# Fixed addresses for the 64 row scatters of a routing stage, in place of a loop that copies their row numbers first

## The chip, the core and the metric

The kernel runs on one core of a Trainium2 chip. The metric is the device time of one execution in microseconds (us), as the median of several runs. The core has five engines with a program each: TensorE (PE, matrix products), VectorE (DVE), ScalarE (ACT), GpSimd (POOL) and SyncE (SP, which here only issues DMAs). They wait for one another through semaphores.

## What is computed

A decoder of two layers on 32 sequences of 128 tokens of width 256. Layer 0 has a gated recurrence, a retention block and a mixture of experts; layer 1 has attention, cross attention on a context, and a memory layer. The change lies in the dispatch of the mixture of experts. Cut to that, the reference is:

```python
logits = xt @ wg                                   # 4096 tokens, 8 experts
scores = softmax(logits)
topv, topi = top_k(scores, 2)
flat = one_hot(topi.T, 8).reshape(2 * N, 8)
pos = sum((cumsum(flat, axis=0) - 1) * flat, -1).reshape(2, N).T
valid = pos < capacity                             # 1024 rows an expert
disp = zeros((8, capacity, 256)).at[topi, where(valid, pos, 0)].add(xt * valid)
y = relu(disp @ w1 + b1) @ w2 + b2                 # per expert
out = sum(gate * y[topi, pos], over the 2 choices)
...
Q = q @ Wq + bq; K = ctx @ Wk + bk; V = ctx @ Wv + bv    # cross attention of layer 1
```

## The kernel before

The work goes in 16 units of two sequences (UNITS = 16, UB = 2). Each stage is a software pipeline over the units: `pipelined` calls a step function per unit, the first ones written out, the rest in a hardware loop that is unrolled 2 or 4 times. `done`, `landed` and `landed4` are waits on semaphores; a DMA adds 16 to its semaphore when it has landed. The order of the work is written by hand, one program for each engine.

**Stage A** computes recurrence, retention and the routing logits, and stores its result x2 to HBM. **The routing stage** follows. VectorE (`r_vector`) turns the logits into a row number of `disp_d` for every token and choice, and writes these into `slot_s` (128 partitions x 2 choices x 32 sequences, L928); tokens over the capacity get a number beyond the bound. Then GpSimd (`r_gpsimd`) does 16 groups, one a unit. A group has four scatters (L1016), one for each of two choices and two sequences; a scatter writes 128 rows of 1 KB from `R["x"]` to the rows of `disp_d` that the numbers name.

**Beside it** run the keys and values of layer 1's cross attention, which need nothing of the routing: SyncE loads a context tile (L995), TensorE transposes it (`to_feature`, L469) and multiplies it by two weights (L477, L485), ScalarE copies the results (L974, L978, L979) and SyncE stores them (L1000). VectorE splits the first expert's weights into parts (L1166, L499, L1170).

**SyncE's program** (`r_sync`) ties the two together. Its step for unit t is, in this order: wait until the context tile of t-2 is transposed and load the context of t; wait for the scatters of unit t-4 (`r_sc`), whose buffer of four is then free, and load x2 of t (L997); wait for ScalarE's copies of t-2 and store its keys and values. SyncE's queue is in order, so one late wait holds up all that follows. After the last step comes `m_sync`, the expert stage: it waits for all 64 scatters (L1072) and loads the first tile of `disp_d` (L1078).

**The expert stage** M runs 16 tiles of 512 rows. TensorE waits in its beginning for all stores of keys and values, then for the first tile, transposes it (L1118), and goes on with the products (L504). Nothing of it can start before the last scatter has landed.

The program of the routing stage on GpSimd, on which the change bears:

## Time and profile before

| | us |
|---|---|
| median of 3 runs | 1977.65 |
| lowest and highest run | 1974.51, 1977.91 |
| the profiled execution, its own time | 1973.47 |
| span in its trace | 1971.7 |
| PE, DVE, ACT, POOL busy | 1629.6, 1272.4, 744.0, 525.7 |

The span runs from the first to the last instruction in the trace; 1.8 us of the execution lie around it. Busy time of an engine is an average over stages with different limits, so the rows below are read by stage: stage A ends at about 375 us, the routing stage reaches to about 490 us, the expert stage to about 880 us.

### The profile page before, as it was taken

The numbers are of one execution on the slowest core, as the hardware profiler recorded it, in microseconds if no ns is written. First come the engines' busy times: TensorE is split into PE (matmuls) and PEld (weight loads), VectorE is DVE, ScalarE is ACT, GpSimd is POOL, SyncE is SP. The second block draws the span as 40 slices with busy tenths as digits, with TensorE's granted clock in tenths as the row PEclk, the third lists the DMA queues.
The fourth block names the chain that finished last, engine by engine and source line by source line (L and its number), as shares of the span: only waits on it lengthen the run. The fifth ranks groups of instructions, "written<-read, shape, count | busy, mean of one in ns | idle before, by whom it ended". The sixth has DMA issues, their size and how long they took to land.

```text
span 1971.7 us, 35134 instructions
## 1 busy us (share of the span) xinstructions
PE 1629.6 (83%) x12950; PEld 1429.1 (72%) x12950; DVE 1272.4 (65%) x2542; ACT 744.0 (38%) x1319; POOL 525.7 (27%) x648
## 2 busy tenths in 40 slices
PE   4667777575999999985777769999968999899997
PEld 3556656464898888874566558887847889888897
DVE  4879999620555555525988837876756666665664
ACT  3334444132444444431333324443423333333332
POOL 1223232176000000005555311111103333333333
PEclk8878898698899999997999969999979999999999
DMA  4331110385022222302222231111110000000000
GB/s 164 118 118 33 37 42 26 129 269 206 29 86 86 86 85 91 112 27 86 65 68 82 65 134 61 64 59 55 34 33 1 22 23 12 23 17 17 22 12 17
DMA packets 98603, 133.92 MB, mean 68 GB/s; under 512 B 8562, under 2 KB 83548, under 8 KB 97956
## 3 DMA queue, kind: packets, MB, share of 16 engines
q1 hardware_dynamic: 87716, 107.21, 16.4%
q0 software_dynamic: 6144, 16.41, 2.6%
q10 hardware_dynamic: 4608, 8.39, 1.2%
q8 instruction: 98, 1.61, 0.3%
q14 instruction: 37, 0.30, 0.1%
HBM read 82.02 MB, written 50.33 MB: 67 GB/s over the span
## 4 chain that ended last, share of the span: by engine, by line
PE 31%; issue 11%; DVE 8%; POOL 4%; ACT 1%; DVEq 0%; POOLq 0%; DMA 0%; ACTq 0%
PE psum L504 11%; PE psum L1656 3%; PE psum L1640 3%; POOL d_g_parts L1919 3%; PE psum L1634 2%; PE psum L1617 2%; PE psum L485 2%; PE psum L477 2%; PE psum L1317 1%; DVE arena_y L455 1%; PE psum L469 1%; DVE arena_y L1435 1%; PE psum L1343 1%; DVE arena_y L1429 1%; POOL arena_y L1280 1%
## 5 line engine op out<-in xcount | busy, mean ns | idle before, releaser
L1919 POOL TENSOR_TENSOR d_g_parts<-arena_x,d_g_parts 128x512 fp32r<-128x512 f32 x128 | 164.6, 1286 | 306.4 <-ACT d_g_parts L2010 306.4
L504 PE MATMUL psum<-d_x_parts,d_v_high 128*128 128x256 f32 x1024 | 198.4, 292 | 27.9 <-DVE arena_x L2126 24.8
L504 PE MATMUL psum<-d_v_high,d_g_parts 128*128 128x256 f32 x1024 | 205.9, 284 | 13.0 <-POOL d_g_parts L1919 13.0
L504 PE MATMUL psum<-m_w_high,m_h_parts 128*128 128x256 f32 x1024 | 188.0, 284 | 0.0
L504 PEld LDWEIGHTS psum<-d_x_parts,d_v_high 128*128 128x128 f32 x1024 | 159.9, 193 | 38.7 <-DVE arena_x L2126 28.3
L2126 DVE SCALAR_TENSOR_TENSOR arena_x<-arena_x,psum 128x512 f32<-128x512 f32 x128 | 87.7, 685 | 143.9 <-ACT arena_x L2018 143.7
L504 PEld LDWEIGHTS psum<-d_v_high,d_g_parts 128*128 128x128 f32 x1024 | 167.8, 191 | 16.4 <-POOL d_g_parts L1919 16.2
L1144 ACT ACTIVATE arena_x<-psum,b_e 128x512 f32<-128x512 f32 x128 | 88.2, 689 | 196.5 <-PE psum L504 94.2
L504 PE MATMUL psum<-m_xF_parts,m_w_high 128*128 128x512 f32 x512 | 159.6, 393 | 2.1 <-DVE m_xF_parts L499 2.1
L504 PEld LDWEIGHTS psum<-m_w_high,m_h_parts 128*128 128x128 f32 x1024 | 160.8, 192 | 0.0
L469 PE MATMUL psum<-const,arena_x 128*128 128x128 f32 x448 | 78.8, 312 | 81.1 <-DVE arena_x L455 40.3
L504 PE MATMUL psum<-d_x_parts,d_vd_low 128*128 128x256 f32 x512 | 145.4, 284 | 0.0
L504 PE MATMUL psum<-m_w_low,m_h_parts 128*128 128x256 f32 x512 | 144.9, 283 | 0.0
L504 PE MATMUL psum<-d_vu_low,d_g_parts 128*128 128x256 f32 x512 | 144.6, 282 | 0.0
L2018 ACT ACTIVATE arena_x<-psum 128x512 f32<-128x512 f32 x128 | 76.5, 597 | 177.5 <-PE psum L504 177.5
L469 PEld LDWEIGHTS psum<-const,arena_x 128*128 128x128 f32 x448 | 58.5, 160 | 104.2 <-DVE arena_x L455 46.9
L499 DVE TENSOR_TENSOR m_h_parts<-arena_x,m_h_parts 128x512 fp32r<-128x512 f32 x128 | 84.5, 687 | 44.0 <-ACT m_h_parts L1148 44.0
L504 PEld LDWEIGHTS psum<-m_xF_parts,m_w_high 128*128 128x128 f32 x512 | 96.1, 190 | 21.8 <-issue 2.5
L1709 ACT ACTIVATE arena_x<-psum,arena_x 128x1024 f32<-128x1024 f32 x64 | 71.1, 1110 | 100.8 <-PE psum L1640 100.8
L1286 POOL COPY c_idx_t<-slot_g 128x4 int32<-128x4 int32 (+1 forms) x16 | 2.9, 181 | 395.8 <-POOLq L356 395.8
L1767 DVE TENSOR_REDUCE arena_x<-psum 128x16 f32<-128x2048 f32 x32 | 73.3, 2290 | 53.8 <-PE psum L1617 53.8
L2010 ACT ACTIVATE d_g_parts<-arena_x 128x512 fp32r<-128x512 f32 x128 | 80.1, 626 | 67.4 <-DVE arena_x L2131 67.4
(270 smaller groups left out, 4000.5 us busy)
## 6 DMA issues: line engine op xcount, KB each, us to landing
arena_y<-in_L_ffn_w SPq DMA_DIRECT2D x16, 1024.0 KB, 7.9
arena_x<-x_d SPq DMA_DIRECT2D x48, 256.0 KB, 2.8
arena_x<-in_ctx SPq DMA_DIRECT2D x32, 256.0 KB, 4.0
disp_d<-zeros ACTq DMA_DIRECT2D x32, 256.0 KB, 2.7
x_d<-arena_x SPq DMA_DIRECT2D x32, 256.0 KB, 2.1
kv_d<-arena_x SPq DMA_DIRECT2D x16, 512.0 KB, 3.5
arena_x<-disp_d SPq DMA_DIRECT2D x16, 512.0 KB, 8.5
y_d<-arena_x SPq DMA_DIRECT2D x16, 512.0 KB, 9.3
```

The lines of the kernel that those rows point to most:

```text
L469: ins = nc.tensor.transpose(dst[:, c * T + b * S:c * T + (b + 1) * S], src[:, b, c * P:(c + 1) * P], ident)
L499: return nc.vector.tensor_tensor(dst, src, high.bitcast(F32), ALU.subtract)
L504: ins = nc.tensor.matmul(dst, left[a_], right[b_], start=start and k == 0, stop=stop and k == 2, skip_group_check=True)
L1144: nc.scalar.activation(M["hr"][:, m % 4, :], bank(2 + m % 4), ACT.Relu, bias=b1_e[:, (u.c // 2) % 2, m:m + 1]).then_inc(m_hs, 1)
L1640: ins = nc.tensor.matmul(bank(4 + quad % 2)[:, j * S:(j + 1) * S], X["k"][rows, u.p, par, c * T + b * S:c * T + (b + 1) * S], X["q"][rows, ...
L1656: ins = nc.tensor.matmul(bank(7)[32 * quad:32 * quad + 32, (kind * NC_ + c) * S:(kind * NC_ + c + 1) * S], left, X["eT"][:, b, at:at + S], ...
L1709: nc.scalar.activation(X["eT"][:, b, half * 1024:(half + 1) * 1024].rearrange("p (q n) -> p q n", q=2), psum[:, 4:6, :], ACT.Exp, scale=HD ...
L1767: nc.vector.tensor_reduce(X["mx"][:, b, :].rearrange("p (q j) -> p q j", q=4)[:, :, 0:4], psum[:, 0:4, :].rearrange("p q (k s) -> p q k s" ...
L1919: nc.gpsimd.tensor_tensor(K["gP"][:, s % 2, 1], K["g"][:, s % 2], K["gP"][:, s % 2, 0].bitcast(F32), ALU.subtract).then_inc(d_gl, 1)
L2010: nc.scalar.activation(K["gP"][:, s % 2, 0], K["g"][:, s % 2], ACT.Copy).then_inc(d_gh, 1)
L2018: nc.scalar.activation(K["th"][:, s % 2], bank(s % 2).rearrange("p (k t) -> p k t", k=2), ACT.Tanh, scale=0.5).then_inc(d_th, 1)
L2126: nc.vector.scalar_tensor_tensor(K["t"][:, s % 2], K["th"][:, s % 2], 1.0, z, ALU.add, ALU.mult).then_inc(d_t, 1)
```

## The change

The loop over the units is written out in full. The row numbers are no longer copied into a small tile `R["idx"]`: each scatter reads them where they are, in `slot_s`, which a loop whose position is only known in a register did not do. With the copy go its semaphore `r_idx`, the two `carry` operations around it (one addition of one element each, which give the waits ahead of them an instruction to stand on), and GpSimd's own wait for the scatters of unit t-4. That this wait isn't needed for the buffer follows from SyncE's: x2 of t is loaded into it only when the scatters of t-4 have landed.

```diff
         R["x"] = arena_x.take([P, 4, UB, D])
-        R["idx"] = arena_x.take([P, 4, TOP0, UB]).bitcast(I32)
...
-            def step(t):
-                landed4(pool, r_in, t)
-                landed4(pool, r_sc, t.back(4), 4)
-                carry(pool, 0)
-                nc.gpsimd.tensor_copy(R["idx"][:, t.c % 4], slot_s[:, :, bass.ds(t.n * UB, UB)]).then_inc(r_idx, 1)
-                done(pool, r_idx, t)
-                carry(pool, 1)
+            for u in (Unit(0, n, 4) for n in range(UNITS)):
+                landed4(pool, r_in, u)
                 for c in range(TOP0):
                     for b in range(UB):
+                        at = u.n * UB + b
                         nc.gpsimd.indirect_dma_start(
                             out=disp_d,
-                            out_offset=bass.IndirectOffsetOnAxis(ap=R["idx"][:, t.c % 4, c, b:b + 1], axis=0),
-                            in_=R["x"][:, t.c % 4, b, :], in_offset=None, bounds_check=SLOTS - 1,
-                            oob_is_err=False).then_inc(r_sc[t.c % 4], 16)
-            pipelined(pool, UNITS, 0, step, unroll=4)
+                            out_offset=bass.IndirectOffsetOnAxis(ap=slot_s[:, c, at:at + 1], axis=0),
+                            in_=R["x"][:, u.c % 4, b, :], in_offset=None, bounds_check=SLOTS - 1,
+                            oob_is_err=False).then_inc(r_sc[u.c % 4], 16)
```

GpSimd's order of instructions at the start of the routing stage, before (`r_in_0` is the load of the unit's x2, `r_slots` the end of VectorE's work on the numbers, `s_prefill` the zeroing of `disp_d`):

```order
L463 TENSOR_TENSOR A_st<-A_st,minus_half 128x2 [waits ln2_ag] x2
L513 TENSOR_TENSOR pool_cell<-pool_cell 1x1 [waits r_in_0,r_slots,s_prefill]
L1011 COPY arena_x<-slot_s 128x4
L513 TENSOR_TENSOR pool_cell<-pool_cell 1x1 [waits r_idx]
L1016 DMA disp_d<-arena_x 8192x256 x4
L513 TENSOR_TENSOR pool_cell<-pool_cell 1x1 [waits r_in_1]
L1011 COPY arena_x<-slot_s 128x4
L513 TENSOR_TENSOR pool_cell<-pool_cell 1x1 [waits r_idx]
L1016 DMA disp_d<-arena_x 8192x256 x4
```

The same place of GpSimd's program in the changed kernel, whose scatter is its line 1010:

```order
L463 TENSOR_TENSOR A_st<-A_st,minus_half 128x2 [waits ln2_ag] x2
L1010 DMA disp_d<-arena_x,slot_s 8192x256 [waits r_in_0,r_slots,s_prefill]
L1010 DMA disp_d<-arena_x,slot_s 8192x256 x3
L1010 DMA disp_d<-arena_x,slot_s 8192x256 [waits r_in_1]
L1010 DMA disp_d<-arena_x,slot_s 8192x256 x3
L1010 DMA disp_d<-arena_x,slot_s 8192x256 [waits r_in_2]
L1010 DMA disp_d<-arena_x,slot_s 8192x256 x3
```

Three instructions have gone ahead of each four scatters, and the first wait now stands on the first scatter itself.

A quarter of the loop's body on GpSimd before, with the branch at its end (ISA and REGISTER_ALU work out the address of the copy and the values waited for):

```order
L513 TENSOR_TENSOR pool_cell<-pool_cell 1x1 [waits r_sc_3,r_in_3]
L1011 ISA
L1011 COPY arena_x<-slot_s 128x4
L182 REGISTER_ALU
L513 TENSOR_TENSOR pool_cell<-pool_cell 1x1 [waits r_idx]
L1016 DMA disp_d<-arena_x 8192x256 x4
L171 REGISTER_ALU
L171 COMPARE_AND_BRANCH
L329 UNCONDITIONAL_BRANCH
```

The end of GpSimd's routing stage in the changed kernel:

```order
L1010 DMA disp_d<-arena_x,slot_s 8192x256 [waits r_in_2]
L1010 DMA disp_d<-arena_x,slot_s 8192x256 x3
L1010 DMA disp_d<-arena_x,slot_s 8192x256 [waits r_in_3]
L1010 DMA disp_d<-arena_x,slot_s 8192x256 x3
L329 UNCONDITIONAL_BRANCH
```

Copies, additions, address work and loop branch are gone there, and no scatter waits for an earlier scatter any more. The programs of the other four engines have the same instructions in the same order as before.

## Rows read from the trace of the kernel before

**Rows 1.** The page's first line.

```profile
span 1971.7 us, 35134 instructions
```

**Rows 2.** Busy time by stretch, heading included: routing numbers, scatters, start of M.

```profile
core 0: us, PE busy (x) PEld busy (x) DVE busy (x) ACT busy (x) POOL busy (x), PEclk, DMA share, GB/s
375.00:392.60 17.60, 6.67 (x15) 3.73 (x16) 13.74 (x32) 2.87 (x5) 0.00 (x0) 0.60 0.88 313
392.60:489.40 96.80, 65.84 (x310) 53.98 (x309) 13.03 (x24) 25.18 (x46) 72.25 (x112) 0.92 0.70 242
489.40:498.50 9.10, 1.94 (x8) 1.57 (x8) 1.37 (x3) 1.09 (x2) 0.00 (x0) 0.50 0.43 139
```

**Rows 3.** Timeline of all engines, 488 to 499: start, duration, idle before, its releaser.

```profile
488.35 0.97 POOL L1016 DMA_INDIRECT disp_d<-arena_x  x1 [0.30 <-issue]
490.70 6.15 SPq L1078 DMA_DIRECT2D arena_x<-disp_d  x3
494.51 1.94 PE L1118 MATMUL psum<-const,arena_x 128*128 128x128 f32 x8 [18.74 <-DMA arena_x<-disp_d]
498.55 1.19 PE L504 MATMUL psum<-m_xF_parts,m_w_high 128*128 128x512 f32 x2 [2.10 <-DVE m_xF_parts L499]
```

**Rows 4.** Timeline, GpSimd's first group of scatters.

```profile
392.62 0.24 POOL L513 TENSOR_TENSOR pool_cell<-pool_cell 1x1 f32<-1x1 f32 x1 [22.28 <-DVE slot_s L928]
393.07 0.52 POOL L513 TENSOR_TENSOR pool_cell<-pool_cell 1x1 f32<-1x1 f32 x1
393.98 1.22 POOL L1016 DMA_INDIRECT disp_d<-arena_x  x1 [0.38 <-issue]
```

**Rows 5.** Timeline, one group of GpSimd's loop and the next one's first instruction.

```profile
465.49 0.18 POOL L513 TENSOR_TENSOR pool_cell<-pool_cell 1x1 f32<-1x1 f32 x1
...
466.60 1.02 POOL L1016 DMA_INDIRECT disp_d<-arena_x  x1 [0.55 <-issue]
467.92 0.97 POOL L1016 DMA_INDIRECT disp_d<-arena_x  x1 [0.30 <-issue]
...
470.46 0.97 POOL L1016 DMA_INDIRECT disp_d<-arena_x  x1 [0.30 <-issue]
471.45 0.18 POOL L513 TENSOR_TENSOR pool_cell<-pool_cell 1x1 f32<-1x1 f32 x1
```

**Rows 6.** Everything on line 1016: the 64 scatters, in ns, and their landings.

```profile
L1016 POOL DMA_INDIRECT disp_d<-arena_x x64: 967/974/1488, 394.0 to 488.4; - x64
DMA to landing us min/median/max: 2.2/2.9/4.9
```

**Rows 7.** SyncE's waits from 395 to 480: total, times, longest.

```profile
SPq L997 <- DMA disp_d<-arena_x: 34.8, 10, 4.5
SPq L1000 <- ACT arena_x L979: 26.4, 10, 6.0
```

**Rows 8.** Keys and values: TensorE's transposes of units 3, 7, 15, SyncE's loads and stores.

```profile
401.71 0.66 PE L469 MATMUL psum<-const,arena_x 128*128 128x128 f32 x4 [1.62 <-DMA arena_x<-in_ctx]
422.49 0.66 PE L469 MATMUL psum<-const,arena_x 128*128 128x128 f32 x4 [2.10 <-DMA arena_x<-in_ctx]
468.20 0.66 PE L469 MATMUL psum<-const,arena_x 128*128 128x128 f32 x4 [1.50 <-DMA arena_x<-in_ctx]
468.50 0.37 SPq L997 DMA_DIRECT2D arena_x<-x_d  x1
L1000 SPq DMA_DIRECT2D kv_d<-arena_x x16: 337/368/374, 397.3 to 476.9; - x16
```

**Rows 9.** Landing times of the context loads of line 995.

```profile
DMA to landing us min/median/max: 2.7/4.1/11.3
```

**Rows 10.** Busy time by stretch, columns as in Rows 2: the most loaded one.

```profile
400.00:410.00 10.00, 8.31 (x41) 6.70 (x40) 6.08 (x11) 3.26 (x6) 7.63 (x10) 1.00 0.89 299
```

**Rows 11.** Groups from 392.6 to 489.4: busy us, mean ns.

```profile
L1016 POOL DMA_INDIRECT disp_d<-arena_x x64 | 63.7, 996 | 23.0 <-issue 23.0
L1166 DVE CAST m_piece<-arena_y 128x512 fp32r<-128x512 f32 x8 | 4.1, 513 | 0.2
```

**Rows 12.** Busy time by stretch: TensorE's clock around its return.

```profile
480.00:490.00 10.00, 0.00 (x0) 0.00 (x0) 0.00 (x0) 0.00 (x0) 7.16 (x10) 0.50 0.20 78
500.00:502.00 2.00, 2.00 (x6) 1.61 (x5) 0.00 (x0) 0.45 (x1) 0.00 (x0) 0.50 0.00 0
502.00:504.00 2.00, 2.00 (x8) 1.56 (x8) 0.69 (x1) 1.21 (x3) 0.00 (x0) 0.77 0.00 0
```

1 line of the change is left out of this document (removed).

## The prediction, made before the changed kernel ran

> **What bounds the kernel now.** I read three views in this order. First, busy time by stage, from which the reader is to see whose work fills each stretch. While VectorE works out the row numbers (375 to 392.6 us) GpSimd does nothing. From 392.6 to 489.4 the scatters run: GpSimd is counted busy for 72.25 of 96.8 us, TensorE for 65.84, VectorE for 13.03, and the DMA engines have a share of 0.70 [rows 2]. No engine is full, so the stretch is a chain of steps.
>
> Second, the timeline at its end, which names the chain. The last scatter starts at 488.35 and ends at 489.32; SyncE's first load of the dispatched rows is issued at 490.70; TensorE's first transpose starts at 494.51, after 18.74 us in which it had nothing to do; the first product starts at 498.55 [rows 3]. TensorE's work on keys and values had ended at 494.51 - 18.74 = 475.8, and the last store of keys and values was issued at 476.9, ending at 477.2 [rows 8]. So on the day of this trace only the scatters hold the expert stage: what they finish earlier, it starts earlier, until SyncE's own earlier work, which ends at 477.2, is the next to be late. That is 490.70 - 477.2 = 13.5 us away, and this number matters below.
>
> Third, the timeline of GpSimd. A group of four scatters with its preparation takes 471.45 - 465.49 = 5.96 us [rows 5]. Sixteen of them fill 489.32 - 392.62 = 96.7 us [rows 3, 4]; the first three are slower. Between groups there is no wait: the copy and the two additions follow each other and the scatters at once, so GpSimd runs its own chain from end to end, and its pace is the cost of its instructions.
>
> **The change part by part.** *Inside the loop.* One scatter follows the other after 0.30 us of "issue" and lasts 0.97 us: a pitch of 1.27 us, as from 467.92 to 470.46, two pitches in 2.54 [rows 5]. The gap between the last scatter of a group and the first of the next is 466.60 - 465.49 + 0.01 = about 1.12 us. The two additions and the copy lie in it. Without them it should be the 0.30 that stands between any two scatters; the first scatter of a group also lasts 1.02 in place of 0.97. Saved: 0.82 + 0.05 = 0.87 us at each of 15 boundaries, 13.0 us.
>
> *At the start.* The first addition starts at 392.62, when VectorE has delivered the numbers, and the first scatter at 393.98, 1.36 us later [rows 4]. The new first scatter waits for the same thing; give it the ordinary 0.30 of issue and it starts at 392.92. Saved: 1.06 us.
>
> *What is added.* Each group's first scatter now carries the wait for its x2 itself. No scatter of this trace does that. Bounded from below by nothing, since the wait is long satisfied (x2 of unit 15 is requested at 468.50 [rows 8], its scatters begin some 16 us later). Bounded from above by the largest issue gap ahead of a scatter in the loop, 0.55 against 0.30 [rows 5]: 0.25 x 15 = 3.8 us. I take 0.03 a group, 0.5 us in all, near the lower end, because such a wait is a check of a value that is already there. Reading the numbers out of `slot_s` costs what reading them out of the copy cost: one number a partition both times. Writing the loop out costs nothing that I can see: the first four groups were written out before too, and in them scatters follow at the same 0.30.
>
> *The removed wait for the scatters of t-4* saves nothing of its own, since GpSimd did not idle at it. SyncE still has it, and there it costs 34.8 us over ten times [rows 7]. It shortens there with the faster scatters, which brings x2 and the contexts earlier as well.
>
> *The last scatter's landing.* Before, the last scatter landed when SyncE moved on, at most 490.70 - 488.35 = 2.35 us after its start, with DMA engines almost idle (share 0.20) [rows 3, 12]. Now its neighbours are stores of keys and values, so I use the median of all 64, 2.9 us [rows 6]: 0.5 us given back.
>
> *The sum for GpSimd:* 13.0 + 1.06 - 0.5 - 0.5 = 13.0 us. The first load of the dispatched rows would be issued at 477.7. That is half a microsecond behind SyncE's old end of the keys and values at 477.2, so the two chains meet.
>
> *Where the keys and values go.* While not held by the scatters, they advanced from unit 3 to unit 7 in 422.49 - 401.71 = 20.8 us, 5.2 us a unit; the remaining eight took 468.20 - 422.49 = 45.7 us, 5.7 a unit [rows 8], paced by the old group of 5.96 through SyncE's wait. The new group is 5.10 to 5.13, so 5.2 should hold throughout: eight units save 4 us, and SyncE is free at about 473. So the scatters still end last, by some 4 us. Traffic: the stretch moves 96.8 us x 242 GB/s = 23.4 MB [rows 2]; the most loaded stretch shows 299 GB/s at share 0.89 [rows 10], at which 23.4 MB take 78 us. The new stretch is 83.7 us long, so the load rises to about that of the loaded stretch, in which GpSimd was busy for 7.63 of 10 us, no less than over the whole stretch, and not beyond it.
>
> *VectorE beside it.* VectorE splits weights while the first scatters run (all its work in the stretch is 13.03 us [rows 2]; 8 copies of line 1166 last 513 ns on average). The 64 scatters average 996 ns with a median of 974 and a longest of 1488 [rows 6, 11]: the overlap costs (996 - 974) x 64 = 1.4 us in all. One or two scatters more fall into it now, 0.1 us each: nothing in the sum. The Trainium skill (SBUF — State Buffer, the note on the "DVE blocks DMA" trap) has a rule against this: a VectorE copy in two-port mode keeps GpSimd from writing descriptors, and a DMA that meets one takes some 3.1 us in place of 0.62. By that figure one or two more scatters in the overlap would cost an estimated 2.5 to 5 us and the gain would be 8 to 10.5; by the rows it stays at 13, and I go by the rows.
>
> *TensorE's clock.* After TensorE fell idle at 475.8, its clock is at 0.50 (1.2 GHz) from 480 on, still 0.50 up to 502, and comes back to 2.4 GHz within the next 2 us [rows 12]. TensorE would now idle from about 472 to 481.5, some 9.5 us in place of 18.7. It had fallen by 480 the last time, so I expect the low clock at the restart all the same, at its old cost.
>
> **The result.** The expert stage and everything behind it move forward as a whole: TensorE is busy there nearly throughout, VectorE has the first weights split long before the scatters end, and no later work is tied to the routing stage. The trace's own time, 1973.47 (span 1971.7 [rows 1] and 1.8 around it), would become 1960.5. The median of the runs shown lies 4.2 us above it; carried over, 1977.65 - 13.0 = 1964.6.
>
> **The rivals.** *A, as above*: 10 to 14.5 us less (the upper bound of the wait, or no late landing), 1963 to 1968. Chance 0.65.
>
> *B, keys and values end last.* The new load is dense, and context loads take 4.1 us at the median but up to 11.3 [rows 9]. A cycle of two units holds one such load on its path; 2 us more on each makes 6.2 us a unit, and the 8 last units then end 8 x (6.2 - 5.7) = 4 us after 477.2. SyncE issues the first load at 481, gain 9 to 10: 1968. For it speak that the two chains lie within 4 us of one another; against it, that 400 to 410 had this load already, inside the time in which the pace was 5.2. Chance 0.12.
>
> *C, the clock stays up or comes back earlier.* 4.35 us of products and 1.94 us of transposes run at half speed at the restart [rows 3, 12]; at full speed they would take half, 3 us less: 1961.5. For it, the idle time is halved; against it, that the clock was down 4.2 us after TensorE's last product. Chance 0.12.
>
> *F, VectorE holds up the first scatters.* If each of some 11 scatters that run beside VectorE's 13 us took the longest 1.49 in place of 0.97 [rows 2, 6], 5.7 us would be lost and the gain would be 7: 1970. For it, that such a scatter exists; against it, that VectorE's work did this to the average scatter by only 0.02. The rule of the Trainium skill named above (SBUF — State Buffer) would be at work here. Chance 0.04.
>
> *D, no gain.* The written-out scatters could be slower for a reason that the trace doesn't show at this place, such as late instructions, so that the time moves to "issue". 64 gaps of 0.30 + 0.20 us cancel the gain: 1977. Nothing in the written-out first groups speaks for it. Chance 0.04.
>
> *E, slower, through scatters that back up in the DMA queue.* If they come faster than they drain, each lasts longer at GpSimd. The break-even is a pitch of 96.7 / 64 = 1.51 us. If every scatter lasted the longest 1.49 of the trace, the pitch would be 1.79 and the stretch 114.6 us: 18 us more, 1995. Against it, that SyncE's wait still allows at most four units' buffers, and that a landing takes 2.9 us, about two pitches. Chance 0.03.
>
> **How the numbers follow.** A measurement of this kernel tells about 0.2% (4 us) from no change. Faster by more than that: A, B, C and F, 0.93, less 0.01 for a B gone further: 0.92. Within it: D and that 0.01, less half a point for a D gone beyond: 0.045. Slower: E and that half point: 0.035. The time predicted is that of A, 1964.6. The range takes in C with its lower end and the 3.4 us by which the shown runs differ, and B and F with its upper: 1958.5 to 1970.
>
> **What would show each step.** Right: 64 scatters of 0.97 us with 0.30 between all of them, also at the group boundaries, first start near 392.9, last near 474.8; the first load of dispatched rows near 477.7; TensorE's first transpose near 481.5, with about 9 us idle before it, and its wait put down to that load; keys and values stored by 473; SyncE's waits for scatters much under 34.8 us; unchanged durations after that. Wrong: gaps of 0.5 us at the boundaries (the wait was priced too low), scatters over 1 us in the later part (E, or the lock), GpSimd waiting for x2, or a last store of keys and values after the last scatter's landing (B).

## The result: 10 us slower

| | before | after |
|---|---|---|
| median of 13 runs each on the same chip, us | 1976.22 | 1986.03 |
| lowest and highest | 1970.47, 1981.56 | 1980.59, 1992.93 |
| the profiled execution's own time | 1973.47 | 1980.59 |
| its span | 1971.7 | 1978.8 |

The ratio is 1.0053, with a 95% interval of 1.0039 to 1.0068. The forecast was 1964.6, so it had the wrong sign.

The page and the grouped view of the scatter's line (durations in ns as minimum, median, maximum, then the first and last start; below them what GpSimd sat idle for) say of the changed kernel:

```profile
span 1978.8 us, 35040 instructions
L1010 POOL DMA_INDIRECT disp_d<-arena_x,slot_s x64: 971/972/1221, 391.3 to 497.9; - x64
```

The scatters are as short as before [rows 6], but the last one starts at 497.9. GpSimd's and SyncE's waits in the stretch (line waited at, releaser, total, times, longest) name what is new:

```profile
POOL disp_d L1010 <- DMA arena_x<-x_d: 27.0, 7, 9.9
SPq L998 <- ACT arena_x L977: 41.0, 6, 16.0
```

GpSimd, which never idled for x2 before, waits 27.0 us for it in seven waits. SyncE no longer waits for scatters at all (34.8 us before [rows 7]); it waits for ScalarE, up to 16 us at once. ScalarE's own list of waits says whom it waits for:

```profile
ACT arena_x L976 <- remote: 44.0, 5, 13.5
```

"remote" stands where the trace ties no engine's work to the moment of release. Five waits of this kind make 44 us. Before, the same copies had only waits for TensorE, none over 4.4 us, from 395 to 500:

```profile
ACT arena_x L978 <- PE psum L485: 46.3, 16, 4.4
```

Busy time by stretch (columns as in [rows 2]) shows the whole routing stage, a ten-microsecond piece inside a stall, and the last stretches up to TensorE's restart:

```profile
390.30:501.10 110.80, 68.77 (x306) 56.41 (x304) 12.99 (x24) 24.76 (x46) 63.03 (x64) 0.87 0.59 205
410.00:420.00 10.00, 5.80 (x20) 4.46 (x20) 0.00 (x0) 0.60 (x1) 7.75 (x8) 0.83 0.52 183
502.00:506.00 4.00, 0.03 (x1) 0.06 (x1) 0.00 (x0) 0.00 (x0) 0.00 (x0) 0.76 0.99 310
506.00:510.00 4.00, 1.91 (x8) 1.53 (x9) 1.37 (x3) 1.09 (x2) 0.00 (x0) 0.50 0.21 64
```

The routing stage, from the row numbers (ready at 390.3) to the first load of dispatched rows (501.09), takes 110.8 us. Before it took 490.70 - 392.49 = 98.2. That is 12.6 us more. The DMA engines are less busy than before (0.59 against 0.70), and inside the stall less again, so the stage isn't longer for lack of bandwidth. Outside this stage the two executions differ too: the numbers were ready 2.2 us earlier in the one of after, and the rest, from the first load to the end, is 3.3 us shorter (1477.7 against 1481.0). In the profiled runs below that rest lies between 1474.3 and 1490.9 with no relation to the edits that I can see, so I compare the stage by its own length and the kernels by their medians.

**One stall in the timeline.** Picked lines of all engines around the first one (start, duration, then idle time before it and its releaser):

```profile
405.39 1.89 PE L485 MATMUL psum<-L_xattn_Wv,arena_x 128*128 128x256 f32 x8
407.22 0.60 ACT L976 ACTIVATE arena_x<-psum 128x512 f32<-128x512 f32 x1 [7.71 <-remote]
...
411.55 0.60 ACT L972 ACTIVATE arena_x<-psum 128x512 f32<-128x512 f32 x1 [3.24 <-issue]
413.45 2.85 PE L477 MATMUL psum<-arena_x,L_xattn_Wk 128*128 128x256 f32 x8
416.13 1.46 PE L485 MATMUL psum<-L_xattn_Wv,arena_x 128*128 128x256 f32 x6
418.45 0.38 PE L485 MATMUL psum<-L_xattn_Wv,arena_x 128*128 128x256 f32 x1 [0.86 <-issue]
419.19 0.38 PE L485 MATMUL psum<-L_xattn_Wv,arena_x 128*128 128x256 f32 x1 [0.36 <-issue]
421.47 0.97 POOL L1010 DMA_INDIRECT disp_d<-arena_x,slot_s  x1 [0.30 <-issue]
425.67 0.60 ACT L976 ACTIVATE arena_x<-psum 128x512 f32<-128x512 f32 x1 [13.52 <-remote]
426.92 0.37 SPq L998 DMA_DIRECT2D kv_d<-arena_x  x1
427.95 0.64 SPq L995 DMA_DIRECT2D arena_x<-x_d  x1
432.38 0.97 POOL L1010 DMA_INDIRECT disp_d<-arena_x,slot_s  x1 [9.93 <-DMA arena_x<-x_d]
...
494.09 1.89 PE L485 MATMUL psum<-L_xattn_Wv,arena_x 128*128 128x256 f32 x8
496.10 0.60 ACT L976 ACTIVATE arena_x<-psum 128x512 f32<-128x512 f32 x1 [2.94 <-PE psum L485]
```

Read it from the end. GpSimd idles 9.93 us because x2 arrives late. x2 is late because SyncE, whose queue is in order, issued its load only after the store of 426.92. That store waited for ScalarE's copies, and ScalarE started only at 425.67. Which product did that copy need? TensorE has two banks for them and may be one unit ahead, so products and copies have to be counted. The trace has 16 of each. The copy of 407.22 is the third, for a product that ended at 400.44 + 1.89 = 402.33; the copy of 425.67 is the fourth, and its product had ended at 405.39 + 1.89 = 407.28. The product that ended at 419.57 is the fifth, copied at 427.11. So three hand-overs in a row are late, by 4.9, 18.4 and 7.5 us. ScalarE's copy waits for one thing more, the landing of the store of two units earlier (issued at 398.03), but the trace's records of the semaphores point at TensorE: its update for the fourth product is recorded at 425.56, and the one for the fifth at 425.77. The work was done, and word of it came late.

The last two lines are the same hand-over, the fifteenth, in a quiet place of the same trace: products until 495.98, copy from 496.10, 0.12 us. TensorE itself has unexplained gaps in its fifth product (0.86 and 0.36, put down to "issue"). And the late hand-overs go through 3.2 us after the last scatter before the pause ended (421.47 + 0.97 = 422.44). This order was the first hint that the unbroken row of scatters itself holds up its neighbours.

### The profile page after: what moved, and what is told of

It is laid out like the page before. It is cut to its first block, busy times and chain, and to the rows that moved or that the text cites. A ratio compares the mean times of both kernels' runs of the same rounds, so it can differ in the third digit from the quotient of the medians.

```text
span 1978.8 us, 35040 instructions
## 1 busy us (share of the span) xinstructions
PE 1630.0 (82%) x12950; PEld 1428.7 (72%) x12950; DVE 1272.8 (64%) x2542; ACT 743.6 (38%) x1319; POOL 517.1 (26%) x600
## 4 chain that ended last, share of the span: by engine, by line
PE 30%; issue 11%; DVE 8%; POOL 4%; ACT 1%; DVEq 0%; POOLq 0%; DMA 0%; ACTq 0%
PE psum L504 11%; PE psum L1649 3%; PE psum L1633 3%; POOL d_g_parts L1912 2%; PE psum L1627 2%; PE psum L485 2%; PE psum L1610 2%; PE psum L477 2%; PE psum L1310 1%; DVE arena_y L455 1%; PE psum L469 1%; DVE arena_y L1428 1%; PE psum L1336 1%; DVE arena_y L1422 1%; PE psum L1980 1%
```

## The experiments

The expectations number four theories. **1**: scatters that follow one another without a break hold up what the other engines hand to one another. **2**: GpSimd's removed wait for the scatters of t-4 mattered. **3**: the written-out code itself is slow. **4**: it matters where the row numbers are read from (`slot_s` or a copy). "Stage" is the length from the row numbers to the first load of dispatched rows: 98.2 us before, 110.8 after. "Group" is the median time from one group's first scatter to the next one's: 5.96 us before, and 5.1 after where nothing disturbs it (for e16, whose GpSimd waits in most groups, it is the mean). "Late" counts those of ScalarE's 16 copies of keys (line 976 of the changed kernel) that start more than 0.3 us after the product which they wait for has ended, paired by number as above, with the longest of these delays in us: none before, where the longest is 0.12, and 7 after, up to 18.4. Every kernel was timed in five rounds beside the kernel before.

| run | median us | before us | ratio, 95% interval | stage | group | late |
|---|---|---|---|---|---|---|
| e1_pause_group | 1982.83 | 1972.90 | 1.0059 [1.0035, 1.0082] | 108.2 | 5.2 | 9, 18.6 |
| e2_written_out | 1975.00 | 1972.90 | 1.0009 [0.9990, 1.0028] | 98.1 | 5.97 | 0 |
| e3_wait_back | 1986.13 | 1972.90 | 1.0062 [1.0041, 1.0083] | 111.3 | 5.1 | 7, 15.4 |
| e4_copy_no_wait | 1972.62 | 1972.90 | 0.9994 [0.9975, 1.0014] | 98.3 | 5.96 | 1, 0.9 |
| e5_long_pause | 1978.87 | 1972.44 | 1.0026 [1.0006, 1.0047] | 104.5 | 5.52 | 8, 14.0 |
| e6_copied_once | 1985.64 | 1972.44 | 1.0084 [1.0052, 1.0115] | 110.6 | 5.11 | 7, 21.6 |
| e7_even_pause | 1984.41 | 1972.44 | 1.0061 [1.0040, 1.0081] | 106.2 | 5.4 | 5, 21.4 |
| e8_half_rows | 1980.95 | 1972.44 | 1.0048 [1.0029, 1.0066] | 107.3 | 5.1 | 9, 17.8 |
| e9_own_x2 | 2030.52 | 1972.48 | 1.0269 [1.0234, 1.0305] | 151.9 | 5.12 | 4, 65.4 |
| e10_64_rows | 1980.57 | 1972.48 | 1.0053 [1.0032, 1.0075] | 103.6 | 4.8 | 6, 12.4 |
| e12_no_kv | 1968.10 | 1972.48 | 0.9975 [0.9959, 0.9991] | 91.5 | 5.11 | - |
| e13_before_no_kv | 1975.09 | 1972.48 | 1.0014 [0.9993, 1.0034] | 100.3 | 5.97 | - |
| e11_pause_more | 1977.50 | 1977.30 | 1.0009 [0.9993, 1.0025] | 101.8 | 6.18 | 0 |
| e15_half_scatters | 1964.55 | 1977.30 | 0.9945 [0.9928, 0.9961] | 86.9 | 5.4 | 0 |
| e16_direct | 1958.87 | 1977.30 | 0.9920 [0.9900, 0.9941] | 80.7 | 4.8 | 0 |
| e17_pause_mid | 1970.20 | 1969.76 | 0.9994 [0.9973, 1.0014] | 95.6 | 5.78 | 10, 3.3 |
| e18_direct_row | 1966.43 | 1971.24 | 0.9978 [0.9963, 0.9992] | 91.9 | 5.48 | 0 |
| e19_own_x2_paced | 1971.31 | 1971.24 | 1.0008 [0.9991, 1.0026] | 97.7 | 5.80 | 0 |

The diffs below are cut to the lines that matter; declarations, and the counts of waits that follow from an edit, are left out. Timelines show picked lines.

### Which part of the change does it

**e1_pause_group**: the changed kernel with one addition of one element ahead of each group.

```diff
                 landed4(pool, r_in, u)
+                carry(pool, 8 + u.n)
```

> The changed kernel with one addition of one element on GpSimd ahead of each group of four scatters, nothing else. Theory 1 (an unbroken stream of scatters holds up the other engines; a break in it lets them catch up): the small break takes back most of the loss, so 1966 to 1976 us, and ScalarE's waits put down to 'remote' (44 us in the changed kernel) go under 10. Theory 2 (GpSimd's wait for the scatters of unit t-4 is what mattered) and theory 3 (the written-out code is what costs): as the changed kernel, 1982 to 1990, as neither is touched.

**e2_written_out**: the kernel before with its loop written out; copies, additions and waits stay.

```diff
-            pipelined(pool, UNITS, 0, step, unroll=4)
+            for n in range(UNITS):
+                step(Unit(0, n, 4))
```

> The kernel before with its 16 groups written out in place of the loop; copies, additions and both waits stay. Theory 3 (written-out code): slow, 1982 to 1990 us. Theories 1 and 2: as the kernel before, 1974 to 1978, since the gap of 1.1 us between groups and the wait are both there.

**e3_wait_back**: the changed kernel with GpSimd's wait put back.

```diff
                 landed4(pool, r_in, u)
+                landed4(pool, r_sc, u.back(4), 4)
```

> The changed kernel with GpSimd's wait for the scatters of unit t-4 put back on the first scatter of a group. Theory 2 (the wait): 1966 to 1978 us. Theories 1 and 3: as the changed kernel, 1982 to 1990, as that wait is satisfied three groups ahead and makes no gap between scatters.

**e4_copy_no_wait**: the kernel before, written out, without that wait.

```diff
                 landed4(pool, r_in, t)
-                landed4(pool, r_sc, t.back(4), 4)
-                carry(pool, 0)
+                carry(pool, 8 + t.n)
...
-            pipelined(pool, UNITS, 0, step, unroll=4)
+            for n in range(UNITS):
+                step(Unit(0, n, 4))
```

> The kernel before, written out, with its copies and additions, but without GpSimd's wait for the scatters of unit t-4. Theory 2 (the wait): slow, 1982 to 1990 us. Theory 1 (the stream without breaks): as the kernel before, 1974 to 1978, since the gaps of 1.1 us between groups stay. Theory 3: slow as well, but then the run with the written-out loop and the wait is slow too.

The four fall into two pairs. e2 and e4 are written out and one of them lacks the wait, and both run as the kernel before (stage 98.1 and 98.3). e3 has the wait and is as slow as the changed kernel. So theories 2 and 3 fall. What e2 and e4 have in common is that the copy and the two additions still stand between the groups. A single addition (e1) is not enough: it makes the group 5.2 us, and GpSimd still waits for x2 five times, 17.4 us in all. For theory 1 the expectation was 1966 to 1976 us, and 1982.83 misses it: a break as such does not help, so if the theory holds, the length of the break counts.

### Length of the pause, place of the numbers, size of the rows

**e5_long_pause**: the changed kernel with a memset of 128x512 ahead of each group.

```diff
                 landed4(pool, r_in, u)
+                done(pool, r_pause, u.back(1))
+                nc.gpsimd.memset(zeros[:, :], 0.0).then_inc(r_pause, 1)
```

> The changed kernel with a longer break ahead of each group on GpSimd: it fills the tile of zeros again (128x512, 0.53 us at the kernel's start), so that a group takes some 5.7 to 6 us as before, with the row numbers still read where they are. Theory 1, now with the size of the break in it (the stream has to be thinner than one scatter in 1.3 us): back to 1970 to 1978 us. Theory 4 (what costs is reading the numbers from the large tile instead of the small copy): stays at 1982 to 1990.

**e6_copied_once**: all numbers copied by 16 copies first, then the unbroken row, which reads the copy.

```diff
+            for n in range(UNITS):
+                nc.gpsimd.tensor_copy(R["idx"][:, n], slot_s[:, :, n * UB:(n + 1) * UB]).then_inc(r_idx, 1)
+            pool.wait_ge(r_idx, UNITS)
+            carry(pool, 1)
...
-                            out_offset=bass.IndirectOffsetOnAxis(ap=slot_s[:, c, at:at + 1], axis=0),
+                            out_offset=bass.IndirectOffsetOnAxis(ap=R["idx"][:, u.n, c, b:b + 1], axis=0),
```

> The changed kernel, but GpSimd copies all numbers once, ahead of the first scatter (16 copies, some 3 us), and the 64 scatters then run in one stream and read the copy. Theory 4 (the place of the numbers): the stream without breaks does what was forecast, 1962 to 1972 us. Theory 1 (density of the stream): as the changed kernel or a little above it, 1982 to 1992.

**e7_even_pause**: one addition ahead of every scatter in place of one ahead of every group.

```diff
                     for b in range(UB):
+                        carry(pool, 8 + 4 * u.n + 2 * c + b)
```

> The changed kernel with one addition of one element ahead of every scatter, so that the pitch becomes some 1.4 us and a group 5.6. Theory 1: between the changed kernel and the one before, 1972 to 1982 us, and the engines' late starts mostly gone. Theory 4: 1982 to 1990.

**e8_half_rows**: each scatter writes 512 B of every row; the other halves are left out, and the rows land at half the distance.

```diff
-                            out=disp_d,
+                            out=disp_d.rearrange("s (h d) -> (s h) d", h=2),
...
-                            in_=R["x"][:, u.c % 4, b, :], in_offset=None, bounds_check=SLOTS - 1,
+                            in_=R["x"][:, u.c % 4, b, 0:128], in_offset=None, bounds_check=SLOTS - 1,
```

> The changed kernel with scatters of half rows (512 bytes in place of 1 KB, 128 of them a scatter, written to other rows; the other halves are left out, so the output is not the reference's). Same number of scatters, rows and semaphore updates, half the bytes. If the bytes of scatters beside the loads and stores are what holds the engines up: 1962 to 1974 us. If the number of scatters, rows or updates is: 1982 to 1990, as the changed kernel.

e6 is as slow as the changed kernel although its scatters read a copy. Its stage also holds the 16 copies, so that its first scatter starts 5.5 us after the numbers; but the hold-up is there as before, with 15.8 us of waits for x2 and hand-overs up to 21.6 us late. Theory 4 falls. e8 moves half the bytes, its stage is still 107.3 us and its hand-overs are up to 17.8 us late: the bytes are not it, though its 1980.95 us lies just under what was expected for that case. e5 and e7 show the pace. Both came out slower than theory 1 was given (1978.87 against 1970 to 1978, 1984.41 against 1972 to 1982). From the starts of the scatters one can read after how many groups the first long one comes (the first of over 9 us):

| | group, us | first long group |
|---|---|---|
| after | 5.1 | the 6th, 14.7 us |
| e1_pause_group | 5.2 | the 6th, 15.0 us |
| e3_wait_back, e8_half_rows, e6_copied_once | 5.1 | the 6th, the 6th, the 7th |
| e7_even_pause, e5_long_pause | 5.4, 5.5 | the 9th, the 8th |
| before, e2, e4 | 5.96 | none |

On the whole, the slower the row, the later the first stall; but e5, whose groups are slower than e7's and whose four scatters still follow one another at 1.27 us, stalls a group earlier than e7, whose pauses are spread evenly. That something piles up while the row goes on, and faster at a faster pace, is my reading of this; no row of the trace shows what.

### Without a pause, with fewer rows, without the neighbours

**e9_own_x2**: 16 buffers for x2, all loaded ahead, so that GpSimd never waits for SyncE.

```diff
-        R["x"] = arena_x.take([P, 4, UB, D])
+        R["x"] = arena_x.take([P, UNITS, UB, D])
...
+            for n in range(UNITS):
+                sp.dma_start(R["x"][:, n], x2_u[n]).then_inc(r_in[n % 4], 16)
...
-                    landed4(sp, r_sc, u0.back(4), 4)
-                    sp.dma_start(R["x"][:, u0.c % 4], x2_u[u0.n]).then_inc(r_in[u0.c % 4], 16)
...
-                landed4(pool, r_in, u)
+                pool.wait_ge(r_in[u.n % 4], 64)
```

> The changed kernel with a buffer for each of the 16 units' x2, all loaded ahead of the stage, so that GpSimd never waits for SyncE. Theory 1 (a dense stream holds up the hand-overs of the other engines): the scatters end some 82 us after the first, near 475, without a pause, but keys and values fall behind by more than before and are stored last, at 500 or later; 1980 to 1995 us. If instead the x2 loads were what was late by themselves, and keys and values late through them, both end early: 1962 to 1970.

The 64 scatters now run without a break, from 397.9 to 480.4, and the kernel becomes 58 us slower than before, more than the 1980 to 1995 us expected. Of the four theories only the first allows this. Two of TensorE's products, then ScalarE in the timeline:

```profile
414.77 1.89 PE L485 MATMUL psum<-L_xattn_Wv,arena_x 128*128 128x256 f32 x8
422.44 0.48 PE L485 MATMUL psum<-L_xattn_Wv,arena_x 128*128 128x256 f32 x1 [0.34 <-issue]
...
446.24 0.60 ACT L976 ACTIVATE arena_x<-psum 128x512 f32<-128x512 f32 x1 [29.52 <-remote]
458.21 0.60 ACT L972 ACTIVATE arena_x<-psum 128x512 f32<-128x512 f32 x1 [10.89 <-remote]
488.33 0.60 ACT L976 ACTIVATE arena_x<-psum 128x512 f32<-128x512 f32 x1 [29.52 <-remote]
499.79 0.60 ACT L976 ACTIVATE arena_x<-psum 128x512 f32<-128x512 f32 x1 [4.33 <-PE psum L485]
503.69 0.60 ACT L976 ACTIVATE arena_x<-psum 128x512 f32<-128x512 f32 x1 [2.32 <-PE psum L485]
509.10 0.60 ACT L976 ACTIVATE arena_x<-psum 128x512 f32<-128x512 f32 x1 [2.86 <-PE psum L485]
```

Twice ScalarE stands for 29.5 us. The copy of 446.24 is the third and that of 488.33 the fourth; their products had ended at 414.77 + 1.89 = 416.66 and 422.44 + 0.48 = 422.92, so these hand-overs took 29.6 and 65.4 us. The first comes through in the middle of the row, while the scatters go on; why then, and why both waits are of the same 29.52 us, stays open. The second time ScalarE goes on 8 us after the last scatter ended, and from there a copy of line 976 follows the last one every 4 to 5 us, with its waits put down to TensorE again. The stretches of the same run:

```profile
430.00:440.00 10.00, 0.00 (x0) 0.00 (x0) 0.00 (x0) 0.00 (x0) 7.56 (x9) 0.50 0.24 95
490.00:500.00 10.00, 6.36 (x25) 5.42 (x26) 0.00 (x0) 1.69 (x4) 0.00 (x0) 0.62 0.45 157
```

From 430 to 440 nothing runs but scatters, and the DMA engines are busy for a quarter. In the changed kernel the damage limits itself: a late ScalarE makes x2 late, GpSimd runs dry, and in that pause the late hand-overs come through (425.67 and 427.11 in the stall above).

**e10_64_rows**: each scatter has 64 rows; the upper 64 partitions' rows are left out.

```diff
-                            out_offset=bass.IndirectOffsetOnAxis(ap=slot_s[:, c, at:at + 1], axis=0),
-                            in_=R["x"][:, u.c % 4, b, :], in_offset=None, bounds_check=SLOTS - 1,
+                            out_offset=bass.IndirectOffsetOnAxis(ap=slot_s[0:64, c, at:at + 1], axis=0),
+                            in_=R["x"][0:64, u.c % 4, b, :], in_offset=None, bounds_check=SLOTS - 1,
```

> The changed kernel with scatters of 64 rows in place of 128 (the tokens on the upper 64 partitions are left out, so the output is not the reference's). As many scatters and semaphore updates, half the descriptors. If descriptors or rows load what the engines share, the late hand-overs go and the time is that of whatever ends last, 1955 to 1970 us. If it is the number of scatters or their updates, they come faster than before and it is no better than the changed kernel, 1980 to 1995.

Half the rows make the undisturbed group 4.8 us in place of 5.1, and 21.0 us in six waits for x2 remain; the first long group is the 5th, of 10.9 us. So it goes with the scatters, hardly with what each of them carries.

**e12_no_kv** and its twin **e13_before_no_kv**: the changed kernel and the kernel before, both without TensorE's and ScalarE's work on keys and values. Their loads and stores stay; the stores write a constant.

```diff
+            nc.vector.memset(KV["kv"][:, :, :, :], 0.01).then_inc(kv_s, 1)
...
-                    done(sp, kv_cT, u0.back(2))
+                    landed(sp, kv_in, u0.back(2))
...
-                    done(sp, kv_s, u2, 2)
+                    sp.wait_ge(kv_s, 1)
...
-        add("scalar", kv_scalar)
...
-        add("tensor", kv_tensor)
```

> The changed kernel without the computing of keys and values: TensorE's products and ScalarE's copies of that stage are left out, a constant stands in for them, while SyncE's loads of contexts and stores of keys and values stay, so the DMA traffic is the same (the output is not the reference's). To be compared with its twin made from the kernel before. If the scatters' stream hurts by holding up the hand-overs among TensorE, ScalarE and SyncE (theory 1), the written-out stream now runs its 64 scatters in some 82 us, and this kernel is 10 to 14 us faster than the twin. If it is the DMA traffic itself that cannot take the denser stream, it is no faster than the twin.

> The twin of the run before: the kernel before the change, with the same computing left out. Its scatters were the last to end already, so all theories expect the time of the kernel before within 4 us, 1970 to 1977.

With the neighbours' hand-overs gone, the change does what was forecast, for the most part: e12 is 1975.09 - 1968.10 = 7.0 us faster than its twin (10 to 14 were expected), and its stage 8.8 us shorter (91.5 against 100.3). One long group is left, the 11th, and it lies on SyncE:

```profile
450.11 0.97 POOL L1011 DMA_INDIRECT disp_d<-arena_x,slot_s  x1 [0.30 <-issue]
450.45 0.70 SPq L999 DMA_DIRECT2D kv_d<-arena_x  x1
451.38 0.97 POOL L1011 DMA_INDIRECT disp_d<-arena_x,slot_s  x1 [0.31 <-issue]
454.65 0.00 SPq L994 DMA_DIRECT2D arena_x<-in_ctx  x1
455.36 0.70 SPq L996 DMA_DIRECT2D arena_x<-x_d  x1
458.07 0.97 POOL L1011 DMA_INDIRECT disp_d<-arena_x,slot_s  x1 [5.71 <-issue]
```

SyncE issues nothing from 451.15 to 454.65, then loads x2 at 455.36, and GpSimd goes on at 458.07. It is not one long wait. Besides its DMAs SyncE's program has small register instructions ahead of each. Those ahead of the context load (durations in ns as minimum, median, maximum), in e12 and then in its twin:

```profile
L994 SPq MOVE arena_x<-in_ctx x12: 2/29/708, 397.9 to 465.4; - x12
L996 SPq MOVE arena_x<-in_ctx x12: 29/29/38, 395.0 to 463.6; - x12
```

A move that takes 29 ns in the twin takes up to 708 here. In e12, 20 of SyncE's 76 recorded register instructions last over 0.5 us, all of them between 416 and 457, and none in the twin. Around the long group they start 1.4 us apart, so that from one context load to the next (443.45 to 454.65) SyncE needs 11.2 us, where a group of scatters takes 5.1. So TensorE and ScalarE aren't needed for a stall, and it is not only what engines hand to one another that is slow: so are SyncE's own moves, which wait for nothing.

### What kind of work does it, and from which pace

**e11_pause_more**: a longer pause, the memset of e5 and an addition behind it.

```diff
                 landed4(pool, r_in, u)
+                done(pool, r_pause, u.back(1))
+                nc.gpsimd.memset(zeros[:, :], 0.0).then_inc(r_pause, 1)
+                done(pool, r_pause, u)
+                carry(pool, 8 + u.n)
```

> The changed kernel with a longer pause ahead of each group of scatters: one memset of 128x512 on GpSimd and one addition of one element behind it. The group should take 5.7 to 5.8 us, between the 5.52 of the shorter pause, where the first stall came in group 7, and the 5.96 of the kernel before, where none comes. Dense-stream theory with a threshold just above 5.5: no stall, the stage takes 15 x 0.2 = 3 us less than before (95 us in place of 98), median 0.15% under before. Dense-stream theory with a backlog that grows at any group under 5.96: a first stall in group 9 to 12, the stage takes 99 to 103 us, equal to before or slower. If neither the number of scatters in a time matters but only that each group is followed by a pause, as in the kernel before, the result is that of the first.

**e15_half_scatters**: the scatters of the second choice left out, two memsets (and one of one element) in place of each, so half of the experts' rows stay zero. SyncE waits for half as many scatters.

```diff
                     for b in range(UB):
+                        if c == 1:
+                            for k in range(2):
+                                nc.gpsimd.memset(zeros[:, :], 0.0).then_inc(r_pause, 1)
+                                fills += 1
+                                pool.wait_ge(r_pause, fills)
+                            nc.gpsimd.memset(pool_cell[:, 8 + u.n * 2 + b:9 + u.n * 2 + b], 0.0)
+                            continue
```

> The changed kernel, in which the two scatters of every group's second choice are left out and GpSimd does two memsets of 128x512 and one of one element in place of each (0.55 us a memset, so about as long as a scatter). Half of the rows of the experts' inputs stay zero. GpSimd is as busy and as unbroken as in the changed kernel, with half the scatters. Dense-stream theory (what counts is indirect scatters in a time): no stall of the other engines, no idle time of GpSimd for x2 over 2 us. A theory that any unbroken work of GpSimd on written-out instructions delays the others: the stalls stay, with 2 to 4 idle times of 7 us and more.

**e16_direct**: plain DMAs from GpSimd to fixed rows, so the rows are not dispatched by expert.

```diff
-                        nc.gpsimd.indirect_dma_start(
-                            out=disp_d,
-                            out_offset=bass.IndirectOffsetOnAxis(ap=slot_s[:, c, at:at + 1], axis=0),
-                            in_=R["x"][:, u.c % 4, b, :], in_offset=None, bounds_check=SLOTS - 1,
-                            oob_is_err=False).then_inc(r_sc[u.c % 4], 16)
+                        row = (at * TOP0 + c) * P
+                        nc.gpsimd.dma_start(disp_d[row:row + P, :], R["x"][:, u.c % 4, b, :]).then_inc(r_sc[u.c % 4], 16)
```

> The changed kernel with each scatter replaced by a plain DMA from GpSimd of the same 128 rows of 1 KB to fixed rows of disp_d (so the rows are not dispatched by expert), waits and semaphores as they are. The same 64 transfers, bytes and landings, but no row number is read by GpSimd. If it is the indirect address work that holds up the others, the stalls vanish even at the same pitch, and the stage is bound by keys and values at about 83 to 88 us. If it is any DMA that GpSimd issues back to back, stalls of 7 us and more remain where the pitch is 1.3 us or less; where GpSimd needs longer for such a DMA (a group over 5.9 us) the run doesn't tell.

In e15 GpSimd is busier than in any other version, and nothing stalls: groups of 5.4 us, no idle time for x2. Its stage in the view by stretch:

```profile
392.60:478.40 85.80, 62.98 (x308) 52.04 (x306) 13.71 (x22) 25.30 (x46) 67.74 (x126) 0.96 0.66 227
```

GpSimd is busy for 67.74 of 85.8 us with 126 instructions, and the last store of keys and values is issued at 467.5, earlier than in the kernel before. So it isn't GpSimd's being busy, but how closely and how many scatters follow: here never more than two in a row, and half as many in all.

In e16 the same 64 transfers of 128 KB go in plain DMAs. The view by stretch, GpSimd's waits and one group of its timeline:

```profile
392.60:472.60 80.00, 65.17 (x311) 54.03 (x309) 11.88 (x23) 25.30 (x46) 34.90 (x64) 0.98 0.85 292
POOL disp_d L1011 <- DMA arena_x<-x_d: 38.2, 13, 4.4
438.88 2.14 POOL L1011 DMA_DIRECT2D disp_d<-arena_x  x4 [2.81 <-DMA arena_x<-x_d]
```

The DMA engines are at 0.85 and 292 GB/s, far more than in any stall, and the keys and values advance at 75.0 / 15 = 5.0 us a unit (stores from 397.1 to 472.1). So neither these transfers, their bytes, nor their landings hold up the neighbours. There is a reserve: four plain DMAs take 2.14 us, and from the third group on GpSimd then rests for 1.5 to 4.4 us, so this run doesn't show plain DMAs in an unbroken row; e18, below, does. The Trainium skill (DMA: Bandwidth & Descriptors, "Why a DMA increments its semaphore by 16 and not by 1") says that a DMA from GpSimd posts its semaphore from all 16 engines whatever its shape. That would explain why fewer bytes and rows changed little in e8 and e10, were it these posts that pile up; but e16 posts as many in less time, and stalls nowhere.

e11 came out at 6.18 us a group in place of 5.7 to 5.8, above the old 5.96. It has no stall, as expected, but says nothing of the middle, so one more was run.

**e17_pause_mid**: as e11, its memset cut to 64 columns.

```diff
-                nc.gpsimd.memset(zeros[:, :], 0.0).then_inc(r_pause, 1)
+                nc.gpsimd.memset(zeros[:, :64], 0.0).then_inc(r_pause, 1)
```

> The kernel of the last pause test, with its memset cut from 128x512 to 128x64. The memset of 0.56 us becomes one of about 0.1, so the group becomes 6.18 - 0.46 = 5.7 us, between 5.52 (first stall in group 7) and 5.96 (none). If the backlog grows with the pace, the first stall comes late, in group 9 to 13, and the stage takes 99 to 102 us: equal to before or up to 0.2% slower. If there is a threshold above 5.52 that this kernel passes, no stall comes, the stage takes 15 x 0.25 = 4 us less than before and the median is 0.1 to 0.2% under it.

The scatters, the stores of keys and values, and a row of ScalarE's waits from 385 to 495:

```profile
L1015 POOL DMA_INDIRECT disp_d<-arena_x,slot_s x64: 967/968/1221, 391.0 to 482.5; - x64
L999 SPq DMA_DIRECT2D kv_d<-arena_x x16: 337/368/374, 392.8 to 482.0; - x16
ACT arena_x L977 <- remote: 34.4, 9, 5.2
```

No group is longer than the first (6.3 us); from the third on all 13 are 5.8. So GpSimd begins to stall at a group between 5.52 and 5.78 us. The hold-up itself is not gone, though. The last row has nine waits of ScalarE put down to "remote", and from the seventh on all ten hand-overs are late, by 0.5 to 3.3 us, where none was before. Keys and values advance at (482.0 - 392.8) / 15 = 5.9 us a unit, before at (476.9 - 397.3) / 15 = 5.3: the last store has moved from 476.9 [rows 8] to 482.0, half a microsecond from the last scatter. The two chains have met, 5 us later than in the kernel before. The stage is 2.6 us shorter than before, not the 4 expected without a stall, and too little for the medians to show (0.9994).

### The last two questions: an unbroken row of plain DMAs, a pause without the few buffers

Both start from e9, whose GpSimd never waits for SyncE.

**e18_direct_row**: e9 with a plain DMA to fixed rows in place of each scatter, and a memset of 128x512 behind each.

```diff
-                        nc.gpsimd.indirect_dma_start(
...
+                        row = (at * TOP0 + c) * P
+                        nc.gpsimd.dma_start(disp_d[row:row + P, :], R["x"][:, u.n, b, :]).then_inc(r_sc[u.c % 4], 16)
+                        nc.gpsimd.memset(zeros[:, :], 0.0).then_inc(r_pause, 1)
+                        fills += 1
+                        pool.wait_ge(r_pause, fills)
```

> The kernel with 16 buffers for x2, in which the 64 scatters ran without a break and cost 58 us, with each scatter replaced by a plain DMA from GpSimd of the same 128 rows of 1 KB to fixed rows of disp_d, and a memset of 128x512 on GpSimd behind each, so that the DMAs follow one another at about 1.2 us, the scatters' pitch (rows are not dispatched by expert). GpSimd is unbroken from the first to the last DMA, some 78 us. If any row of DMAs from GpSimd at this pace holds up the others, ScalarE waits up to 29 us again and the kernel is 30 to 60 us slower than before. If it is only the indirect scatter, no wait of ScalarE is over 6 us, keys and values take 5.0 to 5.2 us a unit, the stage is 80 to 86 us and the median 0.6 to 0.9% under before. I expect the second.

**e19_own_x2_paced**: e9 with the pause of e17 ahead of each group.

```diff
                 pool.wait_ge(r_in[u.n % 4], 64)
+                done(pool, r_pause, u.back(1))
+                nc.gpsimd.memset(zeros[:, :64], 0.0).then_inc(r_pause, 1)
+                done(pool, r_pause, u)
+                carry(pool, 8 + u.n)
```

> The same kernel with 16 buffers for x2 and indirect scatters, with the pause of a memset of 128x64 and one addition ahead of each group of four, so that a group takes 5.8 us. GpSimd never waits for SyncE, so nothing but the pause can save the others. If the pause of 0.7 us a group is enough in itself, no wait of ScalarE is over 6 us, the stage is 95 to 96 us and the median equal to before. If the backlog goes on growing at this pace and was only kept down by the few buffers, ScalarE stands for over 10 us somewhere and the kernel is 5 to 50 us slower than before.

The timeline of GpSimd in e18 and ScalarE's waits from 385 to 480:

```profile
420.00 0.54 POOL L1013 DMA_DIRECT2D disp_d<-arena_x  x1 [0.30 <-POOL zeros L1014]
420.53 0.54 POOL L1014 MEMSET zeros<- 128x512 f32 x1
421.37 0.54 POOL L1013 DMA_DIRECT2D disp_d<-arena_x  x1 [0.30 <-POOL zeros L1014]
...
ACT arena_x L977 <- PE psum L485: 46.0, 16, 4.7
```

One DMA follows the other every 1.37 us, four in 5.48, inside the range of paces in which scatters stall the others (5.52 and below), with 0.30 us between GpSimd's pieces of work. Nobody stalls: ScalarE's waits are all for TensorE again, none for products over 4.7 us, and the stores of keys and values go from 405.6 to 476.5, 4.7 us a unit. Its stage, 91.9 us, is that of 64 x 1.37 = 88 us and a later start, since GpSimd waits until 395.03 for the 16 loads; 80 to 86 us had been expected, at a pitch of 1.2. So it takes the indirect scatter. Two things changed with it, however: no row number is read, and the rows go to fixed, consecutive places of `disp_d` instead of scattered ones. Which of the two counts no run tells.

In e19 the same list (395 to 488) has its copies waiting for TensorE alone:

```profile
ACT arena_x L977 <- PE psum L485: 45.7, 16, 4.9
```

Its stage is 97.7 us, where e9's was 151.9. A pause of 0.7 us a group, 15 x 0.7 = 10 us in all, takes away 59 us of loss (2030.52 - 1972.48 = 58.0 against 0.1). It needs no help from the few buffers, and no hand-over is late (0.12 us at most). At the same 5.8 us a group ten were late in e17, whose SyncE also loads x2 during the stage. So the pace alone doesn't fix where the hold-up begins.

## Why the prediction was wrong, step by step

**The reading of before was right.** The scatters alone held the expert stage, and GpSimd's pace was the cost of its instructions. **The gap at the group boundaries** came out as forecast. This is the first scatter of the second group, whose wait for x2 is already met:

```profile
396.71 1.21 POOL L1010 DMA_INDIRECT disp_d<-arena_x,slot_s  x1 [0.30 <-issue]
```

**The added wait** was priced at 0.5 us in all; it costs nothing that the trace shows. **The start** was priced at 1.06 us; the first scatter comes 391.30 - 390.29 = 1.01 us after the numbers, against 393.98 - 392.49 = 1.49 before, so 0.48 was saved, and the gap of 0.30 was the wrong size for an instruction that waits for another engine. The gain of rival A was given as up to 14.5 us; with the term of the wait and that of the landing both at nothing the sum is 14.0. **The removed wait** saves nothing and costs nothing, as said (e3, e4). **VectorE beside it** is right too: from 410 to 420, inside the stall, VectorE has no instruction at all (0.00, x0). The rule of the Trainium skill weighed there (SBUF — State Buffer, the "DVE blocks DMA" trap) can't be at work in that stall; and GpSimd's scatters kept their 0.97 us. **The clock** at the restart was low, as expected: 0.50 from 506, after 6.5 us without a product.

**The step that failed** is "The new group is 5.10 to 5.13, so 5.2 should hold throughout", with its end, "So the scatters still end last, by some 4 us". It took the pace of keys and values from a time when GpSimd's groups took 5.96 us and had 1.1 us without a scatter in each, and carried it over to an unbroken row. I looked for what a denser row does to the traffic and to VectorE, and not for what it does to the waits of the other three engines. e16, e18 and e12 say that the number itself was sound: without that disturbance the keys and values go at 5.0 and 4.7 us a unit (e16, e18), and without them the change gives 7 us (e12). With both side by side, they go at (500.6 - 394.1) / 15 = 7.1 us a unit, the last store comes at 500.58 in place of 473, and GpSimd's x2, behind it in SyncE's queue, costs 27.0 us. The sum closes: from 391.30 to 497.91 are 106.6 us; 63 pitches of 1.27 make 80.0, the pitches of over 2.6 us exceed 1.27 by 24.9 together, and 1.7 are left for the longer first scatters and short waits.

**The rivals.** B had the right end state (keys and values end last, just so: the last store at 500.58 and the first load at 501.09, while the last scatter ended at 498.88) but by late context loads, with 9 to 10 us of gain left. E had the right sign and a mechanism beside it: it let scatters back up and grow longer at GpSimd. They stayed at 972 ns, and those who waited were the neighbours. D, F and C did not occur.

**What is shown and what isn't.** Shown: indirect scatters that follow one another at 1.27 us hold up what TensorE, ScalarE and SyncE hand to one another, at first after nine of them (the product that ended at 402.33, by 4.9 us), then by up to 18.4 us, and by 65.4 in e9. Late hand-overs come through in the middle of a row (407.22; 446.24 in e9) or 3.2 and 8 us after its last scatter. SyncE's own small instructions are slowed as well (e12). The long stalls take no work of VectorE (it did work beside the first late hand-over), no loaded DMA engines and no work on keys and values. The hold-up depends on the scatters' pace, little on their rows and bytes, and plain DMAs from GpSimd at nearly that pace, to fixed rows, don't do it.

Not shown: the resource. The trace has no row for what GpSimd does inside a scatter, such as fetching the numbers, and the delayed hand-overs appear only as "remote" or "issue". Two rivals for it stand. One is the scattered destination itself, as said at e18. The other is the profiler's recording: every time on record comes from an execution with the profiler's span and clock beside it, and in these stretches the trace keeps fewer of the semaphores' updates (544 from 390 to 490 after, 1872 before). Against it as the whole cause, e2 and e4 keep only 918 and 905 and have no hand-over over 0.9 us late; but no run shows the kernel unrecorded.

## What to carry to other kernels

- Before an idle-looking gap on a DMA-issuing engine is closed, ask who hands work over at that time: the 1.1 us of copy and additions between the groups looked like pure cost, and was what let three other engines keep pace. When indirect DMAs from GpSimd run in long rows beside other work, keep a break in them (here a group of four per 5.96 us delayed next to nothing, and one per 5.8 us left small delays in one of two kernels), or put plain DMAs in their place where the rows allow it (the stage takes 80.7 us in e16 against 98.2).
- A stall whose waiter is released several microseconds after the work it waits for has ended ("remote" in the waits) is one of the hand-over. Look at what started or paused at the moment of release, not at the engine named. Pair works and waiters by their number in the program: with two buffers the last work before the release need not be the one that was waited for.
- Where buffers tie the late engine back to the one that disturbs it, the loop hides the size of the effect: only more buffers (e9) showed that an unbroken row costs 58 us and not 10.
- A median equal to before hides small hold-ups. In e17 the kernel's time and GpSimd's row look undisturbed, and ten of 16 hand-overs are late.

## What the runs showed of the hardware

- A row of 64 indirect scatters at 1.27 us held ScalarE for 29.5 us twice, with the DMA engines at 0.24; plain DMAs at 1.37 us, to fixed rows, held nobody. The update of a semaphore for a product that ended at 422.92 was recorded at 488.22.
- With four buffers for x2, GpSimd ran dry in the runs with four scatters per 5.52 us and less, and in none with 5.78 or more. Hand-overs were up to 3.3 us late at 5.79 in e17, and none over 0.12 at 5.79 in e19, at 5.96 before and at 6.18 in e11.
- Beside the unbroken row (e12) register moves of SyncE that take 29 ns took up to 708, and its instructions started 1.4 us apart.
- An indirect scatter costs GpSimd 0.97 us and 0.30 to the next, with 512 B rows as with 1 KB rows; with 64 rows in place of 128 a group of four falls only from 5.1 to 4.8 us. A plain DMA of the same 128 rows costs 0.54 us, four of them 2.14.
